# Causal mask of the row maxima: from mask products on the Tensor engine to a fused add-and-minimum on the Vector engine

## The reference, cut to what matters

```python
scores = jnp.einsum('bkgtd,bksd->bkgts', qg, k) / jnp.sqrt(jnp.asarray(hd, x.dtype))
scores = jnp.where(causal[None, None, None, :, :], scores, jnp.asarray(-jnp.inf, x.dtype))
attn = jax.nn.softmax(scores, axis=-1)
ctx = jnp.einsum('bkgts,bksd->bkgtd', attn, v)
```

## Time and profile before

| quantity | value |
|---|---|
| time, median of 3 runs | 1917.1 us (1910.89 to 1919.61) |
| span of the profiled execution | 1902.1 us |
| PE / DVE / ACT / POOL busy | 94% / 60% / 42% / 29% of the span |
| first attention, 13 units in steady state | 116.7 to 462.1 us |
| second attention, 6 units in steady state | 1489.7 to 1668.4 us |
| DVE busy in these two stretches | 307.65 of 345.4 us, 145.04 of 178.7 us |

### The profile page before, as it was taken

The page is one execution under the profiler, slowest core; times in us unless marked ns, Lnnn a source line. Parts: engine busy times, 40 slices in busy tenths (PEclk is TensorE's granted clock), DMA queues, the critical chain, the costliest instruction groups (busy, mean ns, idle before and its releaser), DMA issues.

```text
span 1902.1 us, 34429 instructions
## 1 busy us (share of the span) xinstructions
PE 1784.1 (94%) x12406; PEld 1130.8 (59%) x12406; DVE 1132.9 (60%) x2233; ACT 803.9 (42%) x1469; POOL 552.9 (29%) x937
## 2 busy tenths in 40 slices
PE   7799999999989999898999999999888999998997
PEld 4334444344469999466999946677543444445774
DVE  6688888888362222776222265744546888836444
ACT  3277777777632322113233211222133676652221
POOL 2322222222221211462121140167242222121670
PEclk9599999999999999989999999999986999999999
DMA  3312222221220000301000050123422121001234
GB/s 112 92 55 60 66 55 56 55 66 45 94 74 23 28 24 21 106 1 55 23 26 26 20 195 1 55 83 104 135 82 64 23 44 32 13 1 55 92 103 147
DMA packets 83176, 114.81 MB, mean 60 GB/s; under 512 B 16808, under 2 KB 61000, under 8 KB 82760
## 3 DMA queue, kind: packets, MB, share of 16 engines
q1 hardware_dynamic: 71880, 82.22, 15.4%
q0 software_dynamic: 11136, 30.42, 5.0%
HBM read 78.33 MB, written 33.69 MB: 59 GB/s over the span
## 4 chain that ended last, share of the span: by engine, by line
PE 78%; DVE 11%; DMA 3%; issue 2%; POOL 2%; ACT 1%; SPq 0%; POOLq 0%; DVEq 0%; ACTq 0%
PE psum L1595 14%; PE psum L1110 11%; PE psum L1094 9%; PE psum L1607 7%; PE psum L1839 5%; PE psum L1055 4%; PE psum L1810 4%; DVE region_a L843 4%; PE psum L1821 2%; PE psum L1858 2%; PE psum L1859 2%; PE psum L1040 2%; PE psum L969 1%; PE psum L1079 1%; PE psum L2286 1%
## 5 line engine op out<-in xcount | busy, mean ns | idle before, releaser
L843 DVE TENSOR_REDUCE region_a<-psum 128x1 f32<-128x640 f32 (+7 forms) x576 | 529.0, 954 | 103.4 <-PE psum L1063 47.5
L947 ACT ACTIVATE region_w<-psum 128x512 f32<-128x512 f32 x864 | 465.4, 601 | 202.4 <-PE psum L1094 198.9
L770 POOL TENSOR_SCALAR_AFFINE_SELECT region_w<-region_w 128x512 f32<-128x512 f32 x192 | 121.8, 635 | 441.7 <-ACT region_w L947 440.0
L1110 PE MATMUL psum<-region_w,region_a 128*32 128x512 f32 (+3 forms) x2304 | 246.8, 501 | 2.2 <-POOL region_w L770 1.2
L1694 DVE TENSOR_TENSOR region_a<-psum,region_a 128x512 f32<-128x512 f32 x76 | 52.5, 691 | 295.9 <-PE psum L1595 295.9
L1094 PE MATMUL psum<-y_norm,region_a 51*128 51x512 bf16 (+1 forms) x612 | 212.0, 389 | 2.9 <-DMA y_norm<-region_a 1.2
L1476 POOL DMA_INDIRECT region_a<-token_rows,region_a x116 | 113.7, 980 | 159.4 <-DVE region_a L1452 82.3
L1094 PEld LDWEIGHTS psum<-y_norm,region_a 51*128 51x128 bf16 (+1 forms) x612 | 55.0, 96 | 161.0 <-ACT region_w L947 116.0
L1595 PEld LDWEIGHTS psum<-region_a,ctx 128*128 128x128 f32 x1280 | 145.9, 192 | 2.5 <-DVE region_a L1669 1.6
L1595 PE MATMUL psum<-region_a,ctx 128*128 128x128 f32 x1280 | 146.3, 275 | 1.1 <-DVE region_a L1669 1.1
L1607 PE MATMUL psum<-region_w,region_a 128*128 x608 | 137.7, 380 | 1.4 <-ACT region_a L1631 1.4
(11 more groups left out here) (239 smaller groups left out, 3064.4 us busy)
## 6 DMA issues: line engine op xcount, KB each, us to landing
y_norm<-a_q SPq DMA_DIRECT2D x132, 64.0 KB
token_rows<-y_norm SPq DMA_DIRECT2D x16, 512.0 KB, 4.8
y_norm<-answer_rows SPq DMA_DIRECT2D x16, 512.0 KB, 6.0
y_norm<-b_q SPq DMA_DIRECT2D x36, 128.0 KB
region_w<-in_f_wg SPq DMA_DIRECT2D x8, 512.0 KB, 3.8
region_w<-in_f_wu SPq DMA_DIRECT2D x8, 512.0 KB, 3.8
region_w<-in_f_wd SPq DMA_DIRECT2D x1, 4096.0 KB, 14.8
region_w<-answer_rows SPq DMA_DIRECT2D x8, 512.0 KB, 8.5
```

Of the source, the lines that this page charges most:

```text
L770: pool.affine_select(p, p, pattern=[[0, GQ], [1, P]], channel_multiplier=-1, base=0, compare_op=ALU.is_ge, fill=0.0)\
L843: dve.tensor_reduce(dst, src, AX_X, ALU.max, negate=True).then_inc(self.ring_done.sem, 1)
L947: act.activation(self.p[col % P_RING][:, :, i % 4, :], c.bank[ST_BANKS[s % 3]].rearrange("p (h t) -> p h t", h=GQ), ACT.Exp, scale=self.sc ...
L1110: mm = pe.matmul(c.bank[ACC_BANK][32 * h:32 * h + 32, P * lo:512], self.vp[slot][:, j, :], self.p[col % P_RING][:, h, lo:4, :], start=(j = ...
```

## The change

A bf16 array `causal` of 1,024 columns per partition holds 896 zeros and then the 128 columns of the mask (0 or -1e30). POOL fills it ahead of the units (one memset, one copy that waits for the mask's load). In `maximum`, one `tensor_tensor_reduce` per head takes the scores from PSUM, adds the last n columns of `causal`, scales by -1, writes the result in bf16 to one of two scratch arrays (`masked_scores`, read by nobody), and keeps the minimum of it, which is the negated maximum, in `mneg`. A step of half 0 has two such instructions, one of half 1 has one. Gone from PE are the mask products: 64 short ones per unit in the first attention, 1,024 in all (L1058, L1060, L1042, L1044), and 32 per unit in the second, 256 in all (L1063). Gone from SP are the two loads of `mq_low` and `ident_low`. The first maximum step of an attention waits for POOL's pads.

```diff
--- before.py
+++ after.py
@@ -492,8 +492,8 @@
         self.mq = r.take([P], BF16)
-        self.mq_low = r.take([P], BF16)
-        self.ident_low = r.take([P], BF16)
+        self.causal = r.take([SEQ], BF16)
+        self.masked_scores = [r.take([SEQ], BF16) for _ in range(2)]
...
@@ -528,11 +528,11 @@
-            self.count(c, "attn", w_in=64, wo_in=16 * (5 if self.max_at else 3),
+            self.count(c, "attn", w_in=64, wo_in=16 * 3,
...
@@ -630,9 +630,6 @@
-        if self.max_at:
-            sp.dma_start(self.mq_low[64:P], d["mq"][0:64, :]).then_inc(self.wo_in.sem, 16)
-            sp.dma_start(self.ident_low[64:P], d["identb"][0:64, :]).then_inc(self.wo_in.sem, 16)
@@ -721,6 +718,7 @@
+        pads += [(self.causal[:, 0:SEQ - P], 0.0)]
@@ -728,8 +726,10 @@
         pool.wait_ge(self.pads.sem, self.pads.at(len(pads)))
-
-        pool.wait_ge(self.wo_in.sem, self.wo_in.at(16 * (5 if self.max_at else 3)))
+        pool.wait_ge(self.wo_in.sem, self.wo_in.at(16 * 3))
+        pool.tensor_copy(self.causal[:, SEQ - P:SEQ], self.mq).then_inc(self.pads.sem, 1)
+        pool.wait_ge(self.pads.sem, self.pads.at(len(pads) + 1))
...
@@ -833,14 +832,17 @@
             both = c.psum[:, bank:bank + 2, :]
-            if half == 0:
-                src, dst = both[:, :, 0:n], self.mneg[0][:, i, h:h + 2]
-            else:
-                src, dst = both.rearrange("p a b -> p (a b)")[:, 0:n], self.mneg[1][:, i - 4, h:h + 1]
...
-            dve.tensor_reduce(dst, src, AX_X, ALU.max, negate=True).then_inc(self.ring_done.sem, 1)
+            if k == 0 and isinstance(u, int) and u == 0:
+                dve.wait_ge(self.pads.sem, self.pads.at(4 + self.slot_pads * SLOTS))
+            for b in range(2 if half == 0 else 1):
+                scores = both[:, b, 0:n] if half == 0 else both.rearrange("p a b -> p (a b)")[:, 0:n]
+                last = dve.tensor_tensor_reduce(
+                    self.masked_scores[k % 2][:, 512 * b:512 * b + n], scores, self.causal[:, SEQ - n:SEQ], scale=-1.0,
+                    scalar=-3.0 * NEG, op0=ALU.add, op1=ALU.min, accum_out=self.mneg[half][:, i - 4 * half, h + b:h + b + 1])
+            last.then_inc(self.ring_done.sem, 1)
...
@@ -1035,33 +1037,19 @@
-                pe.matmul(bank[:, 0:n], qp[hi, h, P * i:P * i + P], kp[hi, 512:512 + n], start=True, stop=False,
+                pe.matmul(bank[:, 0:n], qp[hi, h, P * i:P * i + P], kp[hi, 512:512 + n], start=True, stop=True,
                           skip_group_check=True)
                 pe.matmul(c.bank[self.ring_bank(u, k)][:, :], qp[0:self.krows, h, P * i:P * i + P],
-                          kp[0:self.krows, 0:512], start=True, stop=True, skip_group_check=True)
-                pe.matmul(bank[:, n - P:n], self.ident_low[64:P], self.mq_low[64:P], start=False, stop=False,
-                          skip_group_check=True)
-                pe.matmul(bank[:, n - 64:n], c.identb[64:P, :], self.mq[64:P, 64:P], start=False, stop=True,
-                          skip_group_check=True).then_inc(self.ring.sem, 1)
+                          kp[0:self.krows, 0:512], start=True, stop=True, skip_group_check=True).then_inc(self.ring.sem, 1)
                 return
...
-                if diag and self.max_at:
-                    pe.matmul(bank[:, n - P:n], self.ident_low[64:P], self.mq_low[64:P], start=False, stop=False,
-                              skip_group_check=True)
-                    mm = pe.matmul(bank[:, n - 64:n], c.identb[64:P, :], self.mq[64:P, 64:P], start=False, stop=True,
-                                   skip_group_check=True)
-                elif diag:
-                    mm = pe.matmul(bank[:, n - P:n], c.identb[:, :], self.mq, start=False, stop=True,
-                                   skip_group_check=True)
             mm.then_inc(self.ring.sem, 1)
```

More of the change, by code:

```diff
@@ L534, in __init__ @@
             qk_done=NT, v_done=NT, turned=3 * NG, part1=3 * NG, less1=3 * NG, part2=3 * NG,
-            less2=3 * NG, part3=3 * NG, **{f"parts_out{i}": 16 * self.stores(3 * NG, i) for i in range(PARTS)}, pads=2 + self.slot_pads * SLOTS, vp_in=u, ring=RING_UNIT * u,
+            less2=3 * NG, part3=3 * NG, **{f"parts_out{i}": 16 * self.stores(3 * NG, i) for i in range(PARTS)}, pads=4 + self.slot_pads * SLOTS, vp_in=u, ring=RING_UNIT * u,
             ring_done=RING_UNIT * u, m_neg=8 * u, m_in0=16 * u, m_in1=16 * u,
@@ L783, in gpsimd @@
         pool.wait_ge(self.v_done.sem, self.v_done.at(NT))
-        pool.wait_ge(self.pads.sem, self.pads.at(2 + self.slot_pads * SLOTS))
         copy_v(0, 0)
@@ L1021, in tensor @@
         pe.wait_ge(self.rotm.sem, self.rotm.at(3 * NT if hd == 8 else NT + 1))
-        pe.wait_ge(self.wo_in.sem, self.wo_in.at(16 * (5 if self.max_at else 3)))
+        pe.wait_ge(self.wo_in.sem, self.wo_in.at(16 * 3))
         def max_scores(u, k, slot):
@@ L1050, in max_scores @@
                 head = h + b if half == 0 else h
-                q = qp[lo_row:hi_row, head, P * i:P * i + P]
                 lo = 512 * b * half
                 n = min(512, (i + 1) * P - lo)
-                diag = half == 0 or b == 1
-                mm = pe.matmul(bank[:, 0:n], q, kp[lo_row:hi_row, lo:lo + n], start=True, stop=not diag,
+                mm = pe.matmul(bank[:, 0:n], qp[rows, head, P * i:P * i + P], kp[rows, lo:lo + n], start=True, stop=True,
                                skip_group_check=True)
-                if diag and self.max_at:
-                    pe.matmul(bank[:, n - P:n], self.ident_low[64:P], self.mq_low[64:P], start=False, stop=False,
-                              skip_group_check=True)
-                    mm = pe.matmul(bank[:, n - 64:n], c.identb[64:P, :], self.mq[64:P, 64:P], start=False, stop=True,
-                                   skip_group_check=True)
-                elif diag:
-                    mm = pe.matmul(bank[:, n - P:n], c.identb[:, :], self.mq, start=False, stop=True,
-                                   skip_group_check=True)
             mm.then_inc(self.ring.sem, 1)
```

2 lines of the change are left out of this document (1 added, 1 removed).

## The result

The changed kernel takes 1898.2 us (median of 17 runs, 1888.1 to 1913.8); the kernel before, run beside it, 1913.5 us (17 runs, 1901.0 to 1919.6). The ratio is 0.9946, 95% interval 0.9922 to 0.9969: about 10 us faster, 6 to 15 by the interval. The medians differ by more, 15.3 us, because the times of each kernel lie in two groups: 12 of the 17 runs of the changed kernel are under 1900 us and five are over 1907, while of the kernel before 4 of the 17 are at or under 1905 and 13 over 1909. I had forecast 1935 us, slower, with 1906 to 1975 as the range. The result lies outside it and on the other side; I had given faster a chance of 0.12.

A forecast was written before the change was run, and what follows sets the result against it. PE and DVE were both taken as close to full in the first attention, PE as the bound in the second. First attention +14, second +2, first units +2 made +18 us on 1917.1: 1935 us, range 1906 to 1975.

The forecast's parts named there:

- the price of the fused operation: DVE's maximum steps: 0.15 us beyond the columns per fused operation, between 0.124 and 0.30; 32 per unit make 4.8 us.
- DVE's work plus 1.6: First attention's period: 25.9 us of DVE work a unit plus 1.6 us of DVE waiting taken as staying, 27.5 us.
- The page that I weighed: Skill page on DVE's unavoidable drain: next operation waits for an empty pipeline; a fused operation 0.185 us, kernel near 1955.
- First attention: Its steady units: period 27.5 us, 0.9 more than before; 14 us over the 15 units that overlap.
- my own sign: Steady periods: at or under 26.6 us (first attention) or 28.5 (second) would prove the forecast wrong on the waits.
- Second attention: Its steady units: 30.0 us each, 2 us more in all, with ends of -13 and +10.
- First units: Leading steps of each attention's first units, where PE and DVE alternate: +1 us per attention, 2 in all.
- The base: Whole kernel: median time taken as 15.0 us above the profiled span of 1902.1, carried unchanged, 1917.1 before the change.
- PE's saving decides: Rival, mainly second attention: 13 us saved there, 4 in the first, 1900 us; chance of faster 0.12.
- The tail shows: Rival on DVE: accumulator's write waits for the streaming instruction's full length, 0.21 us a fused operation, +47, 1964 us; chance 0.19.
- It comes out even: Rival: 0.13 us or less a fused operation, about 1 us of waiting left, 1915 us, within 9 either way; chance 0.19.
- The clock: Rival in the steady stretches: PE's waits lower its granted clock, tens of us on top; counted within the high side.

The follow-up runs named there:

- the kernels with memsets: Changed kernel plus a DVE memset behind every fused operation: 64 columns, ratio 1.0028; 128 columns, 1.0336; 128 columns in the first attention alone, 1.0259.

## Why the prediction was wrong

**The step that failed is the price of the fused operation.** The sum had "a fused operation costs 0.15 us beyond its columns"; it is 0.077. I had "excluded" less than 0.124, because each instruction pays the fixed share that all rows show. What was wrong in it is the write, priced at 0.065 us and measured at 0.00 to 0.01: the whole operation costs what a plain reduction costs, 0.074. The rows of independent instructions are all of 64 columns and more; none shows a one-column instruction behind a long one, and that was the case to be priced. Fixed work after the change is 32 x 0.077 = 2.5 us a unit and not 4.8, DVE's work 23.6 and not 25.9. Against the 22.8 of before, that is 0.8 more where the sum had 3.1. At this price DVE no longer sets the first attention's period, so "DVE's work plus 1.6" does not describe it either: it would give 25.2 us, and the period is 26.45, just under the 26.57 of before.

The page that I weighed pointed further the wrong way. Another section of "VectorE: DVE Perf Modes" of the Trainium skill, "Two Vector instructions with no wait between them", says that an operation that writes out its accumulator is two instructions, and that each is held back only if its operands start in another group of 32 partitions than those before it. The maximum steps start at partition 0 throughout, and the trace agrees: 768 writes, and the group of 416 has no idle time and no distance of its own.

**First attention.** Forecast 27.5 us a unit, measured 26.45; with a price near the forecast's put in, 27.4. PE's saving was 0.55, the lower end of my 0.5 to 1.1, and half 1 has no part in it. By my own sign a period at or under 26.6 would have proved me wrong on the waits; the kernels with memsets put the failure on the price instead.

**Second attention.** Forecast 30.0, measured 29.03. PE's saving alone was 1.36, not 1.85: the product's share of the chain overstated it, and why is not shown. I took the value on the losing side because of DVE at 93%; at the true price DVE works 23.6 of 29.0 us and PE waits 16.0 us in 6 units (the waits above). Of the 1.36 saved, 0.61 is lost again.

**First units.** Forecast +1 us each; measured, between the first score products, 43.2 to 42.2 and 46.1 to 45.0: -1 us each. The start of the first attention's first unit came 0.9 us later. The pads cost nothing that can be seen: DVE's first step starts at 59.32 us against 59.24.

**The base.** I took the median as 15.0 us above the profiled span. For the changed kernel that distance is 1.8 us, the difference of time and span in one and the same run. The profiled execution of the kernel before had a short first unit (43.2 us), and by their times the three runs that I took the median of, 1910.9 us and more, were runs with a long one. So of the 37 us by which the forecast missed, 24 lie in the span (1920 against 1896.4) and 13 in this base. The span's own account is: first attention's units -1.6, both first units -2.0 and +0.9 ahead of them, second attention -4.5, and +1.5 in the stages between and after, -5.7 in all. The timed difference is near 10 us. The rest may lie in how often the first unit is short: a mean clock of 0.963 or more had 37 of 53 runs of the four kernels without mask products in half 0 of the first attention (the changed one among them), and 52 of 117 of those with them, and the two kinds of runs of one kernel lie 9 to 15 us apart. The counts show that; why it is so stays open, and the mean clock of a run is only a proxy for the length of its first unit.

**The rivals.** "PE's saving decides" was the right one: a price under 0.13, the gain mostly in the second attention. That its 1900 us lies so near the measured 1898.2 is luck: it had a gain of 13 + 4 us, the units show 4.5 + 1.6, and the difference is made up by the base, which was too high. "The tail shows" is refuted by the start-to-start distances. "It comes out even" came near in the first attention (26.3 us a unit against 26.45), but gave the second nothing. "The clock" is shown to exist, with 12 to 16 us for each long stretch, but only in kernels where DVE is fuller than the change makes it.

## What to carry to other kernels

A second, one-column instruction behind a long one on DVE should be priced by what it moves in the distance of starts, here 0 to 0.01 us, not by its length or by the fixed share of wide instructions. When a trace cannot show an operation, the value below all rows of other shapes is to be kept in the range. Where two engines hand work through a short ring, filling the slower one costs twice: by its own time, and, in the kernels here with DVE filled further, by PE's clock.

## What the hardware showed

- An add with minimum from PSUM (fp32) and SBUF (bf16) into SBUF (bf16) takes 1.042 ns a column and lasts what a plain reduction lasts (1223 against 1222 ns at 1,024 columns); its accumulator's write of 83 ns adds at most 0.01 us between starts (0.077 to 0.083 us beyond the columns, against 0.074 for the reduction).
- A memset behind it adds 0.009 us with 1 column. With 64 and 128 columns (fp32) it adds 0.017 and 0.083 us where DVE works without a break, and 0.08 and 0.145 behind the first operation after a wait.
- With the same program and the same steady units, runs fall into two groups 9 to 15 us apart, and profiles show one first unit of 41.5 to 44.5 or of 53 to 57 us, by how long the clock stays at half; the runs differ by up to 61 us when DVE is filled further.
